# A router's four of eight chosen by rank instead of by four rounds of maximum, in a fused attention and mixture-of-experts block on one core

## The reference

```python
scores = softmax(xt @ gate_w.T)                 # 8 experts for each token
topv, topi = top_k(scores, 4)                   # the four largest; of equal ones, the lower index
topv = topv / sum(topv)
combine = zeros(t, 8).at[token, topi].set(topv) # weight of every expert, 0 for the four not chosen
yexp = (silu(x @ w1[e]) * (x @ w3[e])) @ w2[e]  # every expert for every token
routed = einsum(combine, yexp)                  # plus two shared experts without a weight
```

## Time and profile before

| | |
|---|---|
| median of the three runs | 1153.3 us (1145.38 to 1154.67) |
| the profiled execution's own time | 1154.31 us |
| its span in the trace | 1152.6 us |
| TensorE clock granted, mean of the span | 0.969 |
| DVE busy | 903.6 us (78%) |
| PE busy | 1030.0 us (89%) |
| ACT, POOL busy | 665.7 us (58%), 512.3 us (44%) |

### The profile page before, as it was taken

How to read it: one execution, slowest core, us unless ns; L and a number is a source line. 1 busy time by engine, 2 the same in 40 slices (tenths; PEclk the granted TensorE clock), 3 DMA queues, 4 the chain that set the end, 5 groups by cost and what they waited for, 6 DMA issues and landing times.

```text
span 1152.6 us, 23833 instructions
## 1 busy us (share of the span) xinstructions
PE 1030.0 (89%) x7766; PEld 721.8 (63%) x7766; DVE 903.6 (78%) x2107; ACT 665.7 (58%) x1651; POOL 512.3 (44%) x477
## 2 busy tenths in 40 slices
PE   6776888899998789999998989989998999899997
PEld 4554565566665556666665657657776677677774
DVE  5885677899985667887798877898889887877764
ACT  2543455556655566767675755646675665555563
POOL 2074154503334542132212237858886554466551
PEclk9997899999998999999999999989999999999997
DMA  9997133323333332222222233232533052214320
GB/s 301 354 399 106 56 123 108 124 76 102 107 104 101 97 94 74 69 77 74 64 72 63 56 108 111 74 101 70 139 103 101 12 158 83 80 54 115 104 71 18
DMA packets 87047, 124.00 MB, mean 108 GB/s; under 512 B 11280, under 2 KB 70160, under 8 KB 82832
## 3 DMA queue, kind: packets, MB, share of 16 engines
q1 hardware_dynamic: 76688, 97.30, 28.1%
q0 software_dynamic: 10240, 25.18, 7.6%
HBM read 71.32 MB, written 51.13 MB: 106 GB/s over the span
## 4 chain that ended last, share of the span: by engine, by line
PE 50%; DVE 27%; ACT 9%; issue 8%; another core or an unknown queue 5%; DMA 0%; DVEq 0%; POOL 0%; SPq 0%; ACTq 0%; POOLq 0%
PE bank L1433 6%; PE wide L1457 6%; PE bank L1719 5%; PE bank L1517 5%; PE bank L1709 5%; PE wide L1709 5%; DVE epp L1795 4%; PE bank L1501 3%; DVE kvw L1802 3%; DVE att L1559 2%; PE bank L1509 2%; PE bank L1420 2%; PE bank L1447 1%; ACT epp L1770 1%
## 5 line engine op out<-in xcount | busy, mean ns | idle before, releaser
L1672 POOL TENSOR_TENSOR kvw<-kvw,hq 128x512 f32<-128x512 f32 x128 | 171.3, 1338 | 150.7 <-ACT kvw L1762 150.4
L261 POOL DMA_INDIRECT routed_rows<-hq,idxs x128 | 131.2, 1025 | 232.5 <-DVE att L1559 98.7
L921 POOL DMA_INDIRECT gst<-attended_rows,idxs x128 | 135.2, 1057 | 203.4 <-DVE att L1559 100.2
L1559 DVE SCALAR_TENSOR_TENSOR att<-reach,endrel,wide 128x1024 f32<-128x1024 f32 x152 | 194.4, 1279 | 22.3 <-PE wide L1457 12.6
L1795 DVE TENSOR_TENSOR epp<-kvw,epp 128x512 fp32r<-128x512 f32 x160 | 142.9, 893 | 77.7 <-ACT epp L1770 75.6
L1719 PE MATMUL bank<-epp,w2p 128*128 128x512 f32 x480 | 162.7, 448 | 8.3 <-DVE epp L1795 8.1
L1770 ACT ACTIVATE epp<-kvw 128x512 fp32r<-128x512 f32 x160 | 100.8, 630 | 94.6 <-DVE kvw L1802 89.9
L1709 PE MATMUL bank<-hp,w1p 128*128 128x512 f32 x480 | 140.3, 401 | 0.0
L1709 PE MATMUL wide<-hp,w3p 128*128 128x512 f32 x480 | 138.5, 397 | 0.0
L1433 PE MATMUL bank<-kvw,turned 128*128 x304 | 131.1, 513 | 5.7 <-ACT turned L1321 2.7
L1762 ACT ACTIVATE kvw<-bank 128x512 f32<-128x512 f32 x160 | 94.7, 592 | 57.0 <-PE wide L1709 55.9
(11 more groups left out here) (265 smaller groups left out, 1876.6 us busy)
## 6 DMA issues: line engine op xcount, KB each, us to landing
hq<-weight_rows SPq DMA_DIRECT2D x16, 2048.0 KB
rows<-routed_rows SPq DMA_DIRECT2D x76, 256.0 KB
routed_rows<-zero SPq DMA_DIRECT2D x2, 7168.0 KB
attended_rows<-ob SPq DMA_DIRECT2D x76, 128.0 KB
routed_rows<-zero SPq DMA_DIRECT2D x1, 5120.0 KB, 19.2
out<-fin SPq DMA_DIRECT2D x16, 256.0 KB, 2.4
routed_rows<-hq,idxs POOLq DMA_INDIRECT x128
gst<-attended_rows,idxs POOLq DMA_INDIRECT x128
```

Of the source, the lines that this page charges most:

```text
L261: pool.indirect_dma_start(hs[s], bass.IndirectOffsetOnAxis(idxs[:, t, k:k + 1], 0), hq[:, t, :], None, bounds_check=BLOCKS[s] * P - 1, oob ...
L921: pool.indirect_dma_start(gst[:, u, k, :], None, orow[s], bass.IndirectOffsetOnAxis(idxs[:, t, k % TOPA:k % TOPA + 1], 0), bounds_check=BL ...
L1559: dve.scalar_tensor_tensor(out=att[:, n % 2, :, :], in0=reach[:, :, :].rearrange("p a c -> p (a c)").unsqueeze(1) .to_broadcast([P, 4, 2 * ...
L1672: pool.tensor_tensor(g, g, rows_of(1 - b % 2, n, n + 1), ALU.mult).then_inc(s_eu, 1)
```

## The change

The four rounds are replaced by a count of ranks. For every pair (e, f) of the eight experts one comparison `logit[f] >= logit[e]` is made, kept only where f is less than e (`lower`, a constant 8 x 8 mask in bf16), and the resulting bits are summed along f (`behind`) and along e (`ahead`). `behind - ahead + eslot` (eslot is 8 - e) is then the rank of an expert, from 1 to 8, and those below 5 are kept. This takes 8 x 8 bits for each tile, so it is done for eight tiles at a time: 512 values per partition, in bf16, in the room of two of the five old buffers. The instructions of a group fall from 33 to 16.

```diff
-        left, one, equal, picked, ex = (choice[:, i, :, :] for i in range(5))
+        lower_bit = choice[:, 0:2, :, :].rearrange("p a t e -> p (a t e)").bitcast(BF16) \
+            .rearrange("p (t e f) -> p t e f", e=E, f=E)
+        behind, ahead, ex = (choice[:, i, :, :] for i in range(2, 5))
+        lower = kept("lower", [P, E, E], BF16)
-        MASKS = 17 + 2 * NS
+        MASKS = 19 + 2 * NS
+            link(pool.memset(lower[:, :, :], 1.0))
+            link(pool.affine_select(out=lower[:, :, :], in_=lower[:, :, :], compare_op=ALU.is_ge, fill=0.0,
                                     base=-1, pattern=[[1, E], [-1, E]], channel_multiplier=0))
-        PERIOD, GATHER, CHAIN, ROUTE = 10, 18, 10, 33
+        PERIOD, GATHER, CHAIN, ROUTE = 10, 18, 10, 16
-                elif part < 10:
...
+                elif part < 8:
+                    half, step = divmod(part - 2, 3)
+                    tiles = slice(half * RT // 2, (half + 1) * RT // 2)
+                    shape = [P, RT // 2, E, E]
+                    n = 2 + 4 * half
+                    if step == 0:
+                        link(n + 1, dve.tensor_tensor(lower_bit[:, :, :, :],
+                                                      logits[:, tiles, :].unsqueeze(2).to_broadcast(shape),
+                                                      logits[:, tiles, :].unsqueeze(3).to_broadcast(shape), ALU.is_ge))
+                    elif step == 1:
+                        link(n + 2, dve.tensor_tensor(lower_bit[:, :, :, :], lower_bit[:, :, :, :],
+                                                      lower[:, :, :].unsqueeze(1).to_broadcast(shape), ALU.mult))
+                        link(n + 3, dve.tensor_reduce(behind[:, tiles, :], lower_bit[:, :, :, :], AX.X, ALU.add))
                     else:
+                        link(n + 4, dve.tensor_reduce(ahead[:, tiles, :],
+                                                      lower_bit[:, :, :, :].rearrange("p t e f -> p t f e"), AX.X,
+                                                      ALU.add))
+                elif part == 8:
+                    link(11, dve.tensor_tensor(behind[:, :, :], behind[:, :, :], ahead[:, :, :], ALU.subtract))
+                    link(12, dve.tensor_tensor(behind[:, :, :], behind[:, :, :],
+                                               eslot[:, :].unsqueeze(1).to_broadcast([P, RT, E]), ALU.add))
+                elif part == 9:
+                    dve.wait_ge(s_x1, r + 1)
+                    link(13, dve.scalar_tensor_tensor(out=ex[:, :, :], in0=behind[:, :, :], scalar=float(TOPF + 1),
+                                                      in1=ex[:, :, :], op0=ALU.is_lt, op1=ALU.mult))
                 elif part == 10:
-                    dve.wait_ge(s_x1, r + 1)
-                    link(30, dve.tensor_tensor(ex[:, :, :], ex[:, :, :], picked[:, :, :], ALU.mult))
-                    link(31, dve.tensor_reduce(m, ex[:, :, :], AX.X, ALU.add))
+                    link(14, dve.tensor_reduce(m, ex[:, :, :], AX.X, ALU.add))
+                    link(15, dve.reciprocal(m, m))
                 else:
-                    link(32, dve.reciprocal(m, m))
```

More of the change, by code:

```diff
@@ L568, in routing_gpsimd @@
                                     base=-1, pattern=[[1, E], [-1, E]], channel_multiplier=0))
+            link(pool.memset(lower[:, :, :], 1.0))
+            link(pool.affine_select(out=lower[:, :, :], in_=lower[:, :, :], compare_op=ALU.is_ge, fill=0.0,
+                                    base=-1, pattern=[[1, E], [-1, E]], channel_multiplier=0))
             link(pool.memset(tri[:, :], 1.0))
@@ L1113, in route @@
                     link(2, dve.tensor_tensor(ex[:, :, :], logits, mb, ALU.subtract))
-                elif part < 10:
[L1115 to L1123, removed]
-                    else:
[L1125 to L1132, removed]
@@ L1133, in route @@
                 elif part == 10:
-                    dve.wait_ge(s_x1, r + 1)
-                    link(30, dve.tensor_tensor(ex[:, :, :], ex[:, :, :], picked[:, :, :], ALU.mult))
-                    link(31, dve.tensor_reduce(m, ex[:, :, :], AX.X, ALU.add))
+                    link(14, dve.tensor_reduce(m, ex[:, :, :], AX.X, ALU.add))
+                    link(15, dve.reciprocal(m, m))
                 else:
-                    link(32, dve.reciprocal(m, m))
                     if r:
                         dve.wait_ge(s_wt, r)
-                    link(33, dve.tensor_tensor(wq[:, :, :, :].rearrange("p b e i -> p b i e"),
+                    link(16, dve.tensor_tensor(wq[:, :, :, :].rearrange("p b e i -> p b i e"),
```

## The result

Over 20 runs each, the changed kernel takes 1143.89 us (median; lowest 1131.69, highest 1148.67) and the kernel before 1152.29 us (1143.26 to 1157.83). The ratio is 0.9926, 95% interval 0.9901 to 0.9952: 8.4 us, or 0.7%, faster. In a second series on one chip, beside three experiments, the ratio was 0.9949 (0.9919 to 0.9979). The forecast was 1141 us.

The account below looks back on a forecast made before the run. The prediction took DVE as the bound in the expert stage's router stretches. Groups 1 and 2 at -4.0 us each, group 3 at -2.9 and group 0 at -1.3 made 1153.3 - 12.2 = 1141 us, 8-in-10 range 1131 to 1150.

Parts of the forecast that it names:

- the line at 1%: Border between faster and within: 11.5 us, or 1141.8 us; chances faster 0.47, within 0.45, slower 0.08.
- DVE is the bound in the groups: Expert-stage router stretches: in group 1 a slot's time is the sum of what stands in DVE's program.
- Holding: DVE instructions reading SBUF on both inputs, or the copy, wait for POOL's product; one new holding of 0.95 us allowed.
- Groups 1 and 2: First two expert-stage router stretches: 10.5 us removed, 5.0 and 0.65 added, one holding allowed, -4.0 us each.
- stepped sum: Sum of 512 values read at 16-byte steps: taken at 0.71 us with gap, 1.09 kept for the range.
- Group 3: Last expert-stage router stretch: -5.7 us by DVE's sum, limited by a 17.84 us floor and payback to -2.9 us.
- Group 0: Attention-stage router: 2.5 us less DVE work, of which less than two thirds shows, -1.3 us.
- Moved at no cost: Mask and ACT wait go from part 10 to 9, reciprocal from 11 to 10; over 28 us of cover.
- the two added mask instructions: POOL's mask chain at the start: about 0.5 us longer, costing nothing with 19 us of cover.
- Rival 2: Groups 1 to 3: two more holdings of 0.95 us each, stepped sums at 1.09; -4 us, 1149 us, chance 0.24.
- Rival 3: Router's stepped sums: 16-byte read steps cost much more, 2.5 us per sum decides; slower, chance 0.06.

Follow-up runs that it names:

- e4_plain_sum: Changed kernel with its second sum reading the bits in the order they lie instead of at 16-byte steps; ratio to the kernel before 0.9920.
- e3_later_groups: Rank counting in groups 1 to 3 (expert stage) only, the four rounds of the kernel before kept in group 0; ratio to the kernel before 0.9920.
- e1_layout: Kernel before with only the 128-byte constant mask `lower` and its two POOL instructions added, router unchanged; ratio 1.0032, expert stage 443.64 us.
- a0_changed: The changed kernel itself, run again in a second series; ratio to the kernel before 0.9949, expert stage 435.62 us.
- e5_wide_product: Changed kernel with the constant mask in f32 instead of bf16, so the product has one 32-bit operand; ratio to the kernel before 0.9944.
- f1_shift_256: Changed kernel with another 128 bytes per partition unused behind `lower`, later buffers 256 bytes further than before; ratio to the kernel before 0.9910, expert stage 432.55 us.
- f2_best: Changed kernel with the 256-byte shift and, in groups 1 to 3, the router's instructions moved to other parts; ratio to the kernel before 0.9861.
- e2_first_group: Rank counting in group 0 (attention stage) only, the four rounds of the kernel before kept in groups 1 to 3; ratio to the kernel before 1.0046.
- after: The changed kernel in its first series of 20 runs; median 1143.89 us, ratio to the kernel before 0.9926.

## Why the prediction was right, point by point

The time lies in the range and the mechanism is the one forecast, but 1141 against 1143.89 us looks nearer than it is. The change brought 8.4 us of the 12.2 forecast, and the kernel before came out 1.0 us lower over 20 runs than over three. By the line at 1% the outcome fell within, to which I had given 0.45, and not under faster, with 0.47.

- **DVE is the bound in the groups, and each removed microsecond counts.** Right. e4_plain_sum gives 0.75 us of time for 0.80 of work, and e3_later_groups carries the whole gain.
- **Holding.** Over the eight units of group 1, what DVE's instructions took above the shortest of their kind (counted from 0.1 us) falls from 5.9 us in e1_layout (old router) to 3.9 in a0_changed (same addresses). The router's own part falls from 3.1 to 0.2, and that of L1795, now L1805, grows from 1.7 to 2.6. So the 3.0 us of holding that I counted as removed were there, and 1.1 us of new holding came back against the 0.95 allowed.
- **Groups 1 and 2, -4.0 each.** Measured -3.1. The term that was mis-sized is the stepped sum: 1.076 us where I took 0.68 for it (1.09 with its gap was my upper bound, from L1141's write). Two of them are 0.8 us. The product, 0.418 where I took 0.68, would give 0.5 back, but half of this is lost where products are held. The Trainium skill, "VectorE: DVE Perf Modes" (tier table), gives two elements per cycle for three 16-bit operands, by which I had estimated 0.45 with the gap. The trace (0.418, 0.45 with its gap) and e5_wide_product agree with it.
- **The stepped read.** I chose the row of the same operation over the row of the same step, and the latter was right: L1141's 0.75 ns more per value; measured 0.78 ns ((1.076 - 0.679) / 512). The Trainium skill, "SBUF — State Buffer" (cachelines), puts a penalty on each access that crosses to a new 16-byte line, and this read agrees with it; its sentence that one can stride for free up to 8 bf16 does not, since this step is 8 bf16.
- **Group 3, -2.9.** Measured -2.55, and the next batch took 0.5 back (the ten units behind it go from 21.29 to 21.79), so -2.0 against my figure, which had the payback in it. With one trace each this is good to 0.7 us, by e3_later_groups.
- **Group 0, -1.3.** At like clock -0.4 to -0.9 by the traces. The size is about half; the slot of part 3 there got longer (3.15 to 3.46 us) as said. Whether any of it shows in the time is open.
- **Moved at no cost.** The earlier wait for ACT and ACT's own delay behaved as forecast: part 2's unit is at 4.70 us before and after.
- **What failed: "the two added mask instructions ... costs nothing".** I priced the instructions of `lower` and not its 128 bytes, which moved later buffers and cost 2.1 us of the expert stage by e1_layout, 3.1 by f1_shift_256. I had no row for that and did not look for one.
- **The sum.** -3.1 -3.1 -2.0 -0.6 +2.1 is -6.7 us, against -12.2 forecast and -8.4 measured (5.5 to 11.4 by the interval). The forecast was high by the stepped sums (2.4 us), the address (2.1), and the smaller gains of groups 0 and 3, less what the short products gave. With 3.1 for the address the sum is -5.7, so the traces explain 6 to 7 of the 8.4 us, and the rest is within the scatter of the times.
- **Rival 2 (holding moves rather than goes), -4 us**, was nearer than I gave it credit for: stepped sums at 1.09 were its second half and true. Its first half, two more holdings for each group, was not: the new holding in group 1 is 1.1 us, about one and not three.
- **Rival 3 falls.** It needed 2.5 us for a stepped sum, 4.7 ns a value in all; measured are 1.076 us, 2.1 ns a value.

## What to carry to other kernels

Where one engine is the bound in a stretch, price a rewrite by the sum of its instructions there. Where the row of the same operation and the row of the same access step disagree, keep both prices; here the row of the same step was right. On VectorE beside a busy GpSimd, count how many instructions read two SBUF operands or copy within SBUF: in these traces they wait for GpSimd's products and reductions do not, and this decides where in the order each may stand. A small new constant also moves everything allocated behind it; if the stretches that the change does not touch get longer by a constant share, another padding tells whether the address does it. And a single trace can hold or lack an event of 1 us that has nothing to do with the change: compare unit by unit before a difference of that size is explained.

## What the runs showed of the hardware that was not expected

- TensorE's pace with fp32r operands of 512 columns depends on where buffers lie, here in 14 traces of this one kernel: three matmuls per 0.685 us with the buffers at their old place or 256 bytes on, per 0.70 us at 128 bytes on, and the last 36 units were at 82.4 us in all five traces of the first kind, at 83.5 in all nine of the second, at a granted clock of 1.00.
- A reduction over bf16 at a step of 16 bytes takes 1.076 us for 512 values, at a step of 2 bytes 0.679.
- A product of 512 values with three bf16 operands takes 0.418 us, with one of them f32 0.687.
- A table load took 1.28 us on ACT, and an exponential between two units with silu cost two of them and 1.5 us of kernel time (part 2's unit, 4.70 against 3.16 us).
- The same ten attention slots took 41.3 us at a granted clock of 1.00 (a0_changed, f1_shift_256, f2_best), 42.3 at 0.96 (e2_first_group) and 45.1 at 0.89 (after), in kernels with the same instructions in this stage. after and a0_changed are the same kernel, so which clock came up changed from run to run.
